# A routed feed-forward on one core: wider slots between the steps of a chunk, and result rows scattered to their tokens by each tile where they were fetched by each chunk

## The chip, the cores and the metric

The kernel runs on one core of one Trainium2 chip. The metric is the device time of one execution in microseconds (us), and the number compared is the median of several runs. Engines: PE is TensorE (PEld its weight loads), DVE VectorE, ACT ScalarE, POOL GpSimd, SP SyncE, which here only issues transfers (SPq is its queue).

## The reference, cut

```python
# x (16,2,104,104), txt (16,512,128); all float32
h = tokenizer(x, gamma, beta, W, b)           # 4 half-patch shifts beside x: 10 planes, normed,
                                              # 8x8 patches -> 169 tokens of 128 per image
h = concatenate([h, txt], axis=1)             # 16 x 681 tokens
z = layernorm(h)
y = p_t * cumsum(p_s * z, axis=1)             # decays per channel along the tokens
h = h + (y @ mix_w.T + mix_b)
z = layernorm(h)
logits = z @ Wg                               # 8 experts
topw, topi = top_k(logits, 2); topw = softmax(topw)
gu = z @ Wgu[e] + bgu[e]                      # for an expert e: 128 -> 512
eo = (silu(g) * u) @ Wd[e] + bd[e]            # 256 -> 128
out = h + sum over a token's 2 experts of topw * eo
```

## The kernel before

There are 16 x 169 image tokens and 16 x 512 text tokens. A **chunk** is 4 tokens on each partition: 7 image chunks (104 partitions, the last with 2 tokens each) and 16 text chunks (128 partitions), 23 in all. The image stage comes first and fills the first 110 us; POOL's last work there is the decayed sums (line 972).

**Steps of a chunk.** Text chunks are loaded, normed, transposed, decayed and summed along the tokens (`text_*`, `norm1`, `z_*`). For every chunk: `mix` (PE) adds the mixed rows; `mixed`, `mixed_stats`, `mixed_var` (DVE) and `norm2` (POOL, lines 966 and 1012) give the second norm's scale and shift; `x_norm` (ACT, line 894) writes the normed rows x2; `x_T`, `logits` (PE, lines 719 and 587), `top_value`, `top_index`, `routing` (DVE), `gate_exp` (POOL, line 1018), `rank` (PE), `place` (DVE, line 1369) and `weights` (DVE) find each token's two experts, its two gate weights and two rows in a buffer in HBM, `xbuf`, in which the rows of one expert lie together. POOL then scatters the normed rows there, one indirect DMA for each of 4 tokens and 2 experts (`scatter`, line 1034, 180 in all).

**Groups and tiles.** Chunks form groups: chunks 0 to 3, 4 to 10, 11 to 17, 18 to 22. When a group's chunks are all scattered, its rows are worked off in **tiles** of 256 rows of one expert: 20, 32, 35 and 27 tiles, 114 in all. For a tile SP loads 128 KB of rows and 386 KB of weights; PE transposes the rows (`tile_T`, line 765), multiplies by gate and up (`gate_up`, two units), then by down (`down`, both line 587); ACT and DVE do silu and product (lines 912, 1476); ACT copies the result rows out of PSUM (`row_keep`, line 919); SP stores them to `ybuf`.

**Results.** When all tiles of a group are stored, POOL fetches each token's two result rows by indirect DMAs (`gather`, line 1048, 180 in all; a waiting gather holds up all that is behind it on POOL), DVE weights and adds them (`combine`, lines 1485 and 1489) and SP stores the output.

**Order.** All engines run in order through one list written out by hand: iterations of 16 slots. `AT` gives each step its slot: `mix=(2, 5)` says that at iteration i, slot 5, chunk i + 2 is mixed. A chunk moves on by one iteration in 16 slots. The tiles of a group are spread over the slots until the next group can begin:

```python
TILE_FROM = [b * SLOTS + 1 for a, b in GROUPS]
TILE_TO = TILE_FROM[1:] + [TILE_FROM[-1] + 2 * KT[-1]]
```

So tiles begin at slots 65, 177, 289 and 369 (counted from iteration 0), and the last ends at 423. A group's gathers lie 6 slots after its last tile and are spread over the next group's tiles; those of the last group follow the last tile alone. A slot has no time of its own: an engine goes on as soon as its next instruction's semaphores allow.

## Time and profile before

| | |
|---|---|
| median of 3 runs | 821.02 us (817.8 to 824.27) |
| the profiled execution, its whole time | 824.18 us |
| its span, first to last instruction | 822.4 us |
| busy in the span | PE 603.9 us (73%), DVE 430.1 (52%), ACT 264.7 (32%), POOL 498.1 (61%) |
| mean granted TensorE clock | 0.835 |

The busy shares are means over stages that differ. An instruction of the indirect kind on POOL counts as busy for about 1 us, and the time until the next one can be issued stands as idle "<-issue"; both occupy POOL.

### The profile page before, as it was taken

The numbers are of one execution on the slowest core, as the hardware profiler recorded it, in microseconds if no ns is written. First come the engines' busy times: TensorE is split into PE (matmuls) and PEld (weight loads), VectorE is DVE, ScalarE is ACT, GpSimd is POOL, SyncE is SP. The second block draws the span as 40 slices with busy tenths as digits, with TensorE's granted clock in tenths as the row PEclk, the third lists the DMA queues.
The fourth block names the chain that finished last, engine by engine and source line by source line (L and its number), as shares of the span: only waits on it lengthen the run. The fifth ranks groups of instructions, "written<-read, shape, count | busy, mean of one in ns | idle before, by whom it ended". The sixth has DMA issues, their size and how long they took to land.

```text
span 822.4 us, 12791 instructions
## 1 busy us (share of the span) xinstructions
PE 603.9 (73%) x3335; PEld 519.1 (63%) x3335; DVE 430.1 (52%) x1708; ACT 264.7 (32%) x690; POOL 498.1 (61%) x520
## 2 busy tenths in 40 slices
PE   3787645327778788698989986999898969999000
PEld 2687634316567576586878875888787758888000
DVE  4789655343556657265655766355544623445122
ACT  2502122112234432244442543254253324444000
POOL 5602327763655756377677776477777767760674
PEclk9998855557789988698997997899999979999555
DMA  7185000126345533565655663667577768984221
GB/s 152 53 290 148 1 0 26 33 90 186 101 127 153 145 104 106 164 194 150 185 169 154 205 198 106 191 202 218 179 214 235 236 197 257 279 279 147 80 77 61
DMA packets 84597, 125.23 MB, mean 152 GB/s; under 512 B 15044, under 2 KB 57792, under 8 KB 84526
## 3 DMA queue, kind: packets, MB, share of 16 engines
q1 hardware_dynamic: 72526, 101.66, 40.9%
q0 software_dynamic: 11520, 22.35, 9.5%
q10 hardware_dynamic: 480, 0.41, 0.4%
q8 instruction: 28, 0.46, 0.3%
q14 instruction: 43, 0.35, 0.1%
HBM read 84.25 MB, written 43.25 MB: 155 GB/s over the span
## 4 chain that ended last, share of the span: by engine, by line
PE 37%; POOL 21%; DVE 14%; issue 13%; DMA 7%; ACT 3%; SPq 3%; POOLq 0%; DVEq 0%; ACTq 0%
PE gu L587 15%; PE dn L587 11%; POOL gat L1048 8%; POOL xbuf L1034 8%; PE mx L587 5%; POOL rs L966 3%; DMA gat<-ybuf,ypos 3%; PE xTp L765 3%; DMA space<-xbuf 2%; DMA space<-in_x_dram 2%; PE tr L587 2%; ACT x L894 1%; PE tr L719 1%; DVE gat L1485 1%; DVE rec L1268 1%
## 5 line engine op out<-in xcount | busy, mean ns | idle before, releaser
L1034 POOL DMA_INDIRECT xbuf<-x,pos x180 | 186.4, 1035 | 112.9 <-DVE pos L1369 56.0
L587 PE MATMUL gu<-space,wts 128*128 128x256 f32 x912 | 246.0, 410 | 9.1 <-DVE space L1476 9.1
L1476 DVE SCALAR_TENSOR_TENSOR space<-gu,wts,space 128x256 f32<-128x256 f32 x228 | 109.1, 482 | 235.7 <-ACT space L912 173.3
L1048 POOL DMA_INDIRECT gat<-ybuf,ypos x180 | 177.7, 987 | 87.9 <-issue 55.5
L912 ACT ACTIVATE space<-gu,wts 128x256 f32<-128x256 f32 x228 | 109.1, 479 | 305.7 <-PE gu L587 305.3
L587 PEld LDWEIGHTS gu<-space,wts 128*128 128x128 f32 x912 | 174.8, 206 | 32.0 <-DVE space L1476 10.9
L587 PEld LDWEIGHTS dn<-wts,space 128*128 128x128 f32 x912 | 127.9, 204 | 14.1 <-DVE space L1476 7.1
L587 PE MATMUL dn<-wts,space 128*128 128x128 f32 x912 | 129.1, 288 | 5.8 <-DVE space L1476 5.8
L765 PE MATMUL xTp<-cst,space 128*128 128x128 f32 x228 | 51.8, 311 | 40.2 <-DMA space<-xbuf 38.1
L765 PEld LDWEIGHTS xTp<-cst,space 128*128 128x128 f32 x228 | 26.7, 154 | 52.6 <-DMA space<-xbuf 40.8
L966 POOL TENSOR_TENSOR rs<-ve,nhalf 128x4 f32<-128x4 f32 (+2 forms) x39 | 40.4, 1036 | 29.7 <-DVE ve L1281 15.2
L906 ACT COPY space<-xTp 128x256 f32<-128x256 f32 x114 | 41.5, 364 | 17.5 <-PE xTp L765 17.5
L919 ACT COPY space<-dn 128x256 f32<-128x256 f32 x114 | 43.7, 383 | 9.4 <-PE dn L587 9.4
L1485 DVE SCALAR_TENSOR_TENSOR gat<-gat,w,space 128x128 f32<-128x128 f32 x64 | 18.2, 346 | 51.8 <-DMA gat<-ybuf,ypos 51.8
L587 PE MATMUL dn<-bdt,ones_r 2*128 2x256 f32 x114 | 44.7, 392 | 0.0
L966 POOL TENSOR_TENSOR irs<-ive,nhalf 104x4 f32<-104x4 f32 (+1 forms) x8 | 7.9, 993 | 46.5 <-DVE ive L1186 43.0
L587 PE MATMUL mx<-mask,tri_r 128*128 128x32 f32 (+2 forms) x23 | 8.5, 368 | 35.6 <-DVE mask L1321 35.6
L587 PE MATMUL mx<-mixT,yT 128*128 128x128 f32 x128 | 32.5, 397 | 2.7 <-DVE need_i L1381 1.7
L587 PEld LDWEIGHTS mx<-mixT,yT 128*128 128x128 f32 x128 | 31.1, 327 | 4.4 <-issue 2.0
L719 PE MATMUL tr<-cst,x 128*128 128x128 f32 (+1 forms) x90 | 19.3, 354 | 17.6 <-ACT x L894 17.6
L894 ACT ACTIVATE x<-space,sh,rs 128x128 f32<-128x128 f32 x64 | 26.4, 487 | 15.0 <-POOL sh L1012 15.0
L587 PEld LDWEIGHTS mx<-mask,tri_r 128*128 128x128 f32 (+1 forms) x23 | 5.5, 238 | 40.5 <-DVE mask L1321 39.9
(198 smaller groups left out, 837.8 us busy)
## 6 DMA issues: line engine op xcount, KB each, us to landing
wts<-wall SPq DMA_DIRECT2D x114, 386.0 KB
space<-xbuf SPq DMA_DIRECT2D x114, 128.0 KB, 2.6
ybuf<-space SPq DMA_DIRECT2D x114, 128.0 KB
xbuf<-zero_rows SPq DMA_DIRECT2D x4, 1024.0 KB, 10.5
xt<-in_txt_dram SPq DMA_DIRECT2D x16, 256.0 KB, 3.0
xbuf<-zero_rows SPq DMA_DIRECT2D x32, 128.0 KB
out_dram<-gat SPq DMA_DIRECT2D x16, 256.0 KB
xbuf<-x,pos POOLq DMA_INDIRECT x180
```

Source lines behind the costliest of these rows:

```text
L587: return nc.tensor.matmul(o, l, r, start=a, stop=z_)
L719: last = nc.tensor.transpose(tr_ps[:, j * p:(j + 1) * p], x2[n % NX2][0:p, j * D:(j + 1) * D], ident[0:p, 0:p])
L765: last = nc.tensor.transpose(xT_ps[:, s * P:(s + 1) * P], xrow[k % NX][:, s * D:(s + 1) * D], ident)
L894: last = nc.scalar.activation(x2[n % NX2][0:p, j * D:(j + 1) * D], h1_of(n)[0:p, j * D:(j + 1) * D], ACT.Identity, bias=sh2[0:p, j:j + 1], ...
L906: copy(xT[k % 2], xT_ps[:, 0:SLOT]).then_inc(W.xs_ok, 1)
L912: nc.scalar.activation(sil[q % 3], gu_ps[q % 3][:, 0:SLOT], ACT.Silu, bias=wts[k % NW][:, W_B + t:W_B + t + 1]).then_inc(W.sil_ok, 1)
L919: copy(yrow[k % NYB], dn_ps[k % 2][:, 0:SUB * D]).then_inc(W.y_row_ok, 1)
L966: tt(out_[0:p, 0:w], var[0:p, 0:w], nhalf[0:p, 0:w], ALU.pow).then_inc(done, 1)
L1034: nc.gpsimd.indirect_dma_start(out=xbuf, out_offset=bass.IndirectOffsetOnAxis(pos[0:p, c:c + 1], 0), in_=x2[n % NX2][0:p, m // 2 * D:(m // ...
L1048: nc.gpsimd.indirect_dma_start(out=gat[b][0:p, (k * W4 + j) * D:(k * W4 + j + 1) * D], out_offset=None, in_=ybuf[g], in_offset=bass.Indire ...
L1476: V.scalar_tensor_tensor(hid[q % 4], gu_ps[q % 3][:, SLOT:2 * SLOT], wts[k % NW][:, W_B + HT + t:W_B + HT + t + 1], sil[q % 3], ALU.add, A ...
L1485: last = V.scalar_tensor_tensor(rows[1][j], rows[1][j], wn[1][j], h1_of(n)[0:p, j * D:(j + 1) * D], ALU.mult, ALU.add)
```

## The change

It does four things.

- **The table of slots.** Steps that stood 1 to 3 slots apart now stand mostly 3 to 5 apart. `x_norm` and `gate_exp` go to the next iteration. A chunk's scatters run over 16 slots from its own slot 15 on; a group's tiles begin 8 slots later (73, 185, 297, 377; the last ends at 431).
- **Rows carry their address.** A row of `xbuf` has 130 elements: 128 values, the gate weight, and the number of the row of a new buffer `results` where its result belongs. `x_copy` (ACT) makes the second copy of the chunk's rows, `weights` (DVE) writes weight and number beside them. The padding rows must have a number too: POOL writes numbers into `zero_rows` (`number_pads`), waits until SP has filled the spare rows of `xbuf` with them, and writes other numbers.
- **Tiles scatter.** `row_keep` multiplies by the gate weight (2 instructions for 1), and POOL scatters the scaled rows to `results` (`scatter_rows`, 2 indirect DMAs per tile, 228 in all), 3 tiles behind. SP loads a chunk's two result rows per token with one plain DMA (`load_results`), DVE adds them with two instructions (`combine`), and the output is stored from the tokens' own buffer. The gathers, `places_of_results` and the stores to `ybuf` are gone.
- **Buffers and places.** Row buffers 5 to 12, result buffers 4 to 8, x2 3 to 4, fetch buffers 4 to 3. `text_y` moves from POOL to DVE. `tile_T` waits for rows and weights together.

```diff
-AT = dict(text_load=(5, 8), ... mix=(2, 5), mixed=(2, 6), ... norm2=(2, 9), x_norm=(2, 12),
-          x_T=(1, 2), ... routing=(1, 15), rank=(0, 1), place=(0, 2), weights=(0, 3))
+AT = dict(text_load=(4, 2), ... mix=(2, 4), mixed=(2, 7), ... norm2=(2, 12),
+          x_norm=(1, 0), x_T=(1, 4), ... routing=(1, 14), gate_exp=(0, 2), rank=(0, 10), place=(0, 12), weights=(0, 13))
-TILE_FROM = [b * SLOTS + 1 for a, b in GROUPS]
+TILE_FROM = [b * SLOTS + 9 for a, b in GROUPS]
+SCATTERS_AT = by_slot([(n * SLOTS + 15 + m * (1 if (n + 1) in [b for a, b in GROUPS] else 2), (n, m))
+                       for n in range(CHUNKS) for m in range(2 * width(n))])
+ROW = D + 2
+    results = nc.dram_tensor("results", (RESULT_ROWS, D), F32, kind="Internal").ap()
...
             load_images(1)
-            sp.wait_ge(W.zero_ok, 1)
+            sp.wait_ge(W.spare_ok, 1)
             for g in range(len(GROUPS)):
                 sp.dma_start(xbuf[ROW0[g] + E * CAP[g]:ROW0[g + 1], :].rearrange("(e p s) d -> p e (s d)", e=E, s=SUB),
-                             zero_rows[:, :].unsqueeze(1).to_broadcast([P, E, SUB * D])).then_inc(W.spare, 16)
+                             zero_rows[:, :].rearrange("p (e c) -> p e c", e=E)).then_inc(W.spare, 16)
...
-                wait(sp, W.xTt_ok, k - NX + 1)
-                sp.dma_start(xrow[k % NX].rearrange("p (s d) -> p s d", s=SUB),
-                             xbuf[bass.ds(row, SLOT), :].rearrange("(p s) d -> p s d", s=SUB)).then_inc(xrow_in[k % NX], 16)
                 wait(sp, W.dn_ok, k - NW + 1)
+                if k >= NX:
+                    sp.wait_ge(yrow_out[(k - NX) % NYB], stored_before(k - NX))
+                sp.dma_start(xrow[k % NX], xbuf[bass.ds(row, SLOT), :].rearrange("(p s) d -> p (s d)", s=SUB)
+                             ).then_inc(tile_in[k % NW], 16)
-            def store_tile(k):
...
+            def load_results(n):
+                b, g, p = n % NG, group_of(n), parts(n)
+                if n == GROUPS[g][0]:
+                    for m in range(TILE0[g + 1] - NYB, TILE0[g + 1]):
+                        sp.wait_ge(yrow_out[m % NYB], stored_before(m))
+                wait(sp, W.sum_ok, n - NG + 1)
+                r0 = n * A_CHUNK
+                sp.dma_start(res[b][0:p, 0:2 * width(n) * D].rearrange("p (j c) -> p j c", j=width(n)),
+                             results[r0:r0 + p * 2 * W4, :].rearrange("(p j k) d -> p j (k d)", p=p, k=2)[:, 0:width(n)]
+                             ).then_inc(res_in[b], 16)
...
             def tile_T(k):
-                pe.wait_ge(xrow_in[k % NX], 16 * (k // NX + 1))
+                pe.wait_ge(tile_in[k % NW], 48 * (k // NW + 1))
...
-                copy(yrow[k % NYB], dn_ps[k % 2][:, 0:SUB * D]).then_inc(W.y_row_ok, 1)
+                for s in range(SUB):
+                    last = nc.scalar.activation(yrow[k % NYB][:, s * D:(s + 1) * D], dn_ps[k % 2][:, s * D:(s + 1) * D], ACT.Copy,
+                                                scale=xrow[k % NX][:, s * ROW + D:s * ROW + D + 1])
+                last.then_inc(W.y_row_ok, 1)
...
-            def gather(n, j, k):
...
+            def scatter_rows(k):
+                pool.wait_ge(W.y_row_ok, k + 1)
+                for s in range(SUB):
+                    place = xrow[k % NX][:, s * ROW + D + 1:s * ROW + D + 2].bitcast(I32)
+                    nc.gpsimd.indirect_dma_start(out=results, out_offset=bass.IndirectOffsetOnAxis(place, 0),
+                                                 in_=yrow[k % NYB][:, s * D:(s + 1) * D], in_offset=None
+                                                 ).then_inc(yrow_out[k % NYB], 16)
+            pool.wait_ge(W.zero_ok, 1)
+            pool.wait_ge(W.seen_zero, 2)
+            number_pads(SPARE_ROW).then_inc(W.spare_ok, 1)
+            pool.wait_ge(W.spare, 16 * len(GROUPS))
+            number_pads(PAD_ROW).then_inc(W.pads_ok, 1)
...
+                    for k, t in units(i, s):
+                        if t == 1:
+                            if k >= 3 and not any(first_of_group(m) for m in range(k - 2, k + 1)):
+                                scatter_rows(k - 3)
+                            if last_of_group(k):
+                                for m in range(k - 2, k + 1):
+                                    scatter_rows(m)
```

**Where the order changes.** First POOL, from the end of the image stage (`space<-space,pow_t` are the decayed sums, `rs`, `sh` are `norm2`, `ex` is `gate_exp`, `xbuf<-x,pos` a scatter). Before, then changed:

```order
L972 TENSOR_TENSOR space<-space,pow_t 128x1040
L966 TENSOR_TENSOR rs<-ve,nhalf 104x4 [waits s_ve2_ok]
L1012 TENSOR_TENSOR sh<-nm,rs 104x4 [waits s_rs2_ok,s_nm2_ok]
L966 TENSOR_TENSOR rs<-ve,nhalf 104x4 [waits s_ve2_ok,s_x2_ok]
L1012 TENSOR_TENSOR sh<-nm,rs 104x4 [waits s_rs2_ok,s_nm2_ok]
L1018 TENSOR_TENSOR ex<-euler,gap 104x4 [waits s_gap_ok]
L1034 DMA xbuf<-x,pos 106496x128 [waits s_x2_ok,s_pos_ok]
```

```order
L991 TENSOR_TENSOR space<-space,pow_t 128x1040
L1063 IOTA zero_rows 128x16 [waits s_seen_zero,s_zero_ok]
L1063 IOTA zero_rows 128x16 [waits s_spare]
L985 TENSOR_TENSOR rs<-ve,nhalf 104x4 [waits s_ve2_ok]
L1031 TENSOR_TENSOR sh<-nm,rs 104x4 [waits s_rs2_ok,s_nm2_ok]
L985 TENSOR_TENSOR rs<-ve,nhalf 104x4 [waits s_ve2_ok,s_x2_ok]
L1031 TENSOR_TENSOR sh<-nm,rs 104x4 [waits s_rs2_ok,s_nm2_ok]
L1037 TENSOR_TENSOR ex<-euler,gap 104x4 [waits s_gap_ok]
L985 TENSOR_TENSOR rs<-ve,nhalf 104x4 [waits s_ve2_ok,s_x2_ok]
L1031 TENSOR_TENSOR sh<-nm,rs 104x4 [waits s_rs2_ok,s_nm2_ok]
L1049 DMA xbuf<-x,pos 106496x130 [waits s_w1_ok,s_meta_ok,s_pos_ok]
```

Two instructions that write `zero_rows`, the second of them behind SP's fills, stand ahead of the first chunk's norm, and the third chunk's norm stands ahead of the first scatter.

Then PE, at the same place (`tr<-cst,x20` transposes x2 of chunk 0, `mx<-mixT` and the line under it mix, `tr<-wg` are the logits, `mx<-mask` and `seen` the ranks). Before, then changed:

```order
L719 MATMUL tr<-cst,x20 128x104 x4
L587 MATMUL mx<-mixT,space 104x128 x4
L587 MATMUL mx<-rows2,ones_r 104x512
L587 MATMUL tr<-wg,x2T 104x8 x4
L587 MATMUL mx<-mask,tri_r 104x32
```

```order
L726 MATMUL tr<-cst,x20 128x104 x4
L596 MATMUL mx<-mixT,space 104x128 x4
L596 MATMUL mx<-rows2,ones_r 104x512
L596 MATMUL tr<-wg,x2T 104x8 x4
L726 MATMUL tr<-cst,x21 128x104 x4
L596 MATMUL mx<-mixT,space 104x128 x4
L596 MATMUL mx<-rows2,ones_r 104x512
L596 MATMUL tr<-wg,x2T 104x8 x4
L596 MATMUL mx<-mask,tri_r 104x32
```

The ranks of chunk 0 now stand behind the transposes and logits of chunk 1 and the mixing of chunk 2.

Last POOL, early in the second group's tiles (`gat<-ybuf,ypos` a gather, `results<-space` a result scatter, `yT` is `text_y`). Before, then changed:

```order
L1004 TENSOR_TENSOR sh<-nm,rs 128x4 [waits s_rs1_ok,s_nm1_ok]
L1034 DMA xbuf<-x,pos 106496x128 x2
L1048 DMA gat<-ybuf,ypos 104x128 [waits s_yrow_out2,s_yrow_out1,s_yrow_out3,s_yrow_out0,s_ypos_ok]
L1034 DMA xbuf<-x,pos 106496x128
L966 TENSOR_TENSOR rs<-ve,nhalf 128x4 [waits s_ve2_ok,s_x2_ok]
L1012 TENSOR_TENSOR sh<-nm,rs 128x4 [waits s_rs2_ok,s_nm2_ok]
L1048 DMA gat<-ybuf,ypos 104x128
L1034 DMA xbuf<-x,pos 106496x128 x3
L1018 TENSOR_TENSOR ex<-euler,gap 128x4 [waits s_w1_ok,s_gap_ok]
L1024 TENSOR_TENSOR yT<-cum,pow_t 128x512 [waits s_mix_ok,s_cum_ok]
```

```order
L1023 TENSOR_TENSOR sh<-nm,rs 128x4
L1057 DMA results<-space 27648x128 x2
L1049 DMA xbuf<-x,pos 106496x130 x2
L1057 DMA results<-space 27648x128 x2
L1049 DMA xbuf<-x,pos 106496x130 x2
L1057 DMA results<-space 27648x128 x2
L985 TENSOR_TENSOR rs<-ve,nhalf 128x4
L1031 TENSOR_TENSOR sh<-nm,rs 128x4
```

Between one norm and the next POOL now issues result scatters in pairs, one pair for each tile, where it issued a gather now and then; `yT` is no longer there.

## Rows read from the trace of the kernel before

**Rows 1.** The page: busy time, share of the span and instructions of each engine.

```profile
PE 603.9 (73%) x3335; PEld 519.1 (63%) x3335; DVE 430.1 (52%) x1708; ACT 264.7 (32%) x690; POOL 498.1 (61%) x520
```

**Rows 2.** Windows: length, busy us of PE, PEld, DVE, ACT, POOL, clock, DMA, GB/s.

```profile
110.00:187.00 77.00, 29.27 (x126) 24.10 (x126) 35.17 (x216) 13.95 (x33) 50.22 (x53) 0.50 0.15 42
187.00:342.00 155.00, 119.35 (x587) 100.80 (x588) 86.66 (x380) 53.42 (x142) 87.61 (x94) 0.82 0.45 134
342.00:514.00 172.00, 153.69 (x813) 130.88 (x811) 102.66 (x446) 70.48 (x191) 126.03 (x130) 0.90 0.57 170
514.00:668.00 154.00, 139.58 (x773) 119.06 (x773) 73.50 (x284) 58.17 (x160) 106.39 (x109) 0.94 0.68 205
668.00:761.00 93.00, 91.28 (x511) 78.34 (x511) 42.14 (x116) 37.32 (x106) 51.70 (x54) 0.96 0.78 242
```

**Rows 3.** Timeline after the last tile: start, length, engine, line, operation, [idle before].

```profile
761.17 0.37 ACT L919 COPY space<-dn 128x256 f32<-128x256 f32 x1 [1.04 <-PE dn L587]
...
764.13 0.95 POOL L1048 DMA_INDIRECT gat<-ybuf,ypos  x1 [27.97 <-DMA ybuf<-space]
...
813.13 0.95 POOL L1048 DMA_INDIRECT gat<-ybuf,ypos  x1 [0.30 <-issue]
...
817.97 0.33 SPq L551 DMA_DIRECT2D out_dram<-gat  x1
```

**Rows 4.** Groups on POOL, 342 to 514 us: busy, mean ns | idle.

```profile
L1034 POOL DMA_INDIRECT xbuf<-x,pos x56 | 58.6, 1046 | 32.9 <-issue 17.8 <-DVE pos L1369 13.9 <-DVE ve L1281 0.9
L1048 POOL DMA_INDIRECT gat<-ybuf,ypos x32 | 33.9, 1059 | 11.2 <-issue 11.2
L966 POOL TENSOR_TENSOR rs<-ve,nhalf 128x4 f32<-128x4 f32 x14 | 14.6, 1044 | 2.6 <-DVE ve L1453 2.2
L1024 POOL TENSOR_TENSOR yT<-cum,pow_t 128x512 f32<-128x512 f32 x7 | 8.9, 1265 | 0.1
```

**Rows 5.** Timeline around the first chunks, POOL and then ACT.

```profile
114.98 1.01 POOL L966 TENSOR_TENSOR rs<-ve,nhalf 104x4 f32<-104x4 f32 x1
...
127.42 1.25 POOL L1034 DMA_INDIRECT xbuf<-x,pos  x1 [1.23 <-DVE pos L1369]
...
116.37 1.65 ACT L894 ACTIVATE x<-h_img,sh,rs 104x128 f32<-104x128 f32 x4 [9.75 <-POOL sh L1012]
...
125.27 1.65 ACT L894 ACTIVATE x<-h_img,sh,rs 104x128 f32<-104x128 f32 x4 [5.70 <-POOL sh L1012]
```

**Rows 6.** Fills of spare rows: SP queue, landing times, a window.

```profile
43.72 7.59 SPq L481 DMA_DIRECT2D xbuf<-zero_rows  x4
...
DMA to landing us min/median/max: 6.6/10.5/12.0
...
48.00:52.00 4.00, 4.00 (x39) 4.00 (x38) 4.00 (x10) 0.00 (x0) 0.00 (x0) 1.00 1.07 372
```

**Rows 7.** Timeline where the first group opens.

```profile
181.99 0.99 POOL L1034 DMA_INDIRECT xbuf<-x,pos  x1 [0.30 <-issue]
...
185.29 0.37 SPq L533 DMA_DIRECT2D space<-xbuf  x1
...
187.30 0.69 PE L765 MATMUL xTp<-cst,space 128*128 128x128 f32 x2 [14.55 <-DMA space<-xbuf]
```

**Rows 8.** Groups on POOL, 187 to 342 us.

```profile
L1034 POOL DMA_INDIRECT xbuf<-x,pos x52 | 54.5, 1048 | 41.2 <-DVE pos L1369 25.2 <-issue 15.7 <-DVE ve L1281 0.3
L966 POOL TENSOR_TENSOR rs<-ve,nhalf 128x4 f32<-128x4 f32 (+1 forms) x14 | 14.3, 1022 | 13.5 <-DVE ve L1453 8.4 <-DVE ve L1281 4.9
...
L1018 POOL TENSOR_TENSOR ex<-euler,gap 128x4 f32<-128x4 f32 (+2 forms) x7 | 7.0, 993 | 5.9 <-DVE gap L1307 5.8
```

**Rows 9.** Groups on POOL, 514 to 668 us.

```profile
L1048 POOL DMA_INDIRECT gat<-ybuf,ypos x55 | 55.0, 1000 | 20.4 <-issue 16.5 <-DMA ybuf<-space 3.8
L1034 POOL DMA_INDIRECT xbuf<-x,pos x40 | 40.6, 1014 | 27.1 <-DVE pos L1369 15.6 <-issue 11.4
```

**Rows 10.** Landing of the text loads, 256 KB each, line 475.

```profile
DMA to landing us min/median/max: 2.8/3.0/3.5
```

254 lines of the change are left out of this document (104 added, 150 removed).

## The prediction, made before the run

> **What bounds the kernel now.** The page's busy line comes first, since it says which engines can be a bound at all: PE 603.9 us of 822.4, POOL 498.1 [rows 1]. Neither is full over the span, so the next view is windows cut by stage [rows 2]. The reader is to see five stretches. From 110 to 187 us there is no tile: PE 29 of 77 us at a granted clock of 0.50, POOL 50. From 187 to 342 us (first group's 20 tiles) PE 119 of 155. From 342 to 514 (32 tiles) PE 154 of 172, POOL 126. From 514 to 668 (35 tiles) PE 140 of 154, POOL 106. From 668 to 761 (27 tiles) PE 91 of 93: PE is the bound. What follows is a tail without PE: the last result row is copied by 761.54, the first of 40 gathers starts at 764.13, the last at 813.13, the last store at 817.97 [rows 3]. So 60.9 us stand behind the last tile, and POOL alone sets them.
>
> What POOL's busy time hides is shown by its groups: beside 92.5 us for 88 indirect DMAs stand 29.0 us of "<-issue" [rows 4]. An indirect DMA thus occupies POOL for 1.05 + 0.33 = 1.38 us in this stretch; alone in the tail it is (813.13 - 764.13) / 39 = 1.256 us [rows 3]. True waits of POOL from 342 to 514 us are only 13.9 + 0.9 + 2.2 = 17.0 us [rows 4]: it is taken for 155 of 172 us, as much as PE. This is the number on which the rest hangs.
>
> **The change, part by part.** The sum is made against the profiled execution's span, 822.4 us.
>
> *The wait for the fills.* POOL now writes numbers, waits until SP's four fills of 1.06 MB have landed, and writes again, all ahead of chunk 0's norm, which started at 114.98, right behind the image sums [rows 5]. SP issued the fills at 43.72, hidden beside the image stage [rows 6]; now it can't before about 115, and everything from the first norm on is queued behind POOL's wait: ACT's x_norm, PE's transposes, DVE's routing. Price: SP took 7.59 us to issue four, the last issue began near 48.4 (it took the rest of the 7.59), and the slowest landed 12.0 us after issue, so at most 48.4 + 12.0 - 43.72 = 16.7 us; 4.26 MB at the 372 GB/s of the window beside them is 11.5 us [rows 6]. I take **+15**, near the upper end, since issue and landing add to the bytes.
>
> By the Trainium skill (DMA: Bandwidth & Descriptors, section on the anatomy of one DMA on the SWDGE path) a transfer costs about 2.0 us plus its bytes over 436 GB/s; for all four as one this is an estimate of 11.8 us, and the sum would be 3 us lower. The landing of 12.0 us for one of four [rows 6] speaks for more.
>
> *The spacing before the first tile.* Chunk 0's ranks now stand on PE behind chunk 1's transposes and logits and chunk 2's mixing, and its first scatter behind chunk 2's norm on POOL. In this stretch chunks follow each other in turns of 125.27 - 116.37 = 8.9 us [rows 5]; norm to first scatter took 127.42 - 114.98 = 12.4 us. The first scatter comes almost a turn later, **+8** (0 if the chunks overlap fully, 10 if the opening waits for weights too). From there to the last scatter before the tiles (127.42 to 182.98, [rows 5, 7]) POOL has the same 32 scatters and is nearly always taken, so no gain there; then 4.3 us to PE's first transpose [rows 7], as before.
>
> *The three stretches with chunks and tiles.* PE's work is what it was. POOL's changes: result scatters come in (2 per tile), gathers go, `text_y` goes to DVE, which is busy half the time and hides 0.7 us more per chunk. ACT's second instruction per tile and `x_copy` lie beside 822.4 - 264.7 = 558 us in which ACT is idle [rows 1]; nothing.
> First stretch: POOL waited 25.2 + 0.3 + 8.4 + 4.9 + 5.8 = 44.6 us [rows 8], so it was taken for 110.4. Now + 40 x 1.35 (1.048 + 15.7/52) = 54.0, less 7 x 1.27 = 8.9 for `text_y`: 155.5 us, all of the stretch. The wider slots take PE's waits away, but not this; with an imperfect fit **+5** (-3 at 1.256 us each, +15).
> Second: 155 taken, + 32 x 1.38 = 44.2, - 8.9 = 190.3 us against a stretch of 172 and PE work of 154: POOL becomes the bound. With 3 us in which it starves while a group opens, **+21** (+3 if each of the 120 costs 1.256; +35 if the old 17 us of waits stay).
> Third: waits 3.8 + 15.6 = 19.4, taken 134.6, + 15 x 1.30 = 19.5, - 2 x 1.27 = 2.5, so 151.6 of 154 [rows 9]; PE needs 140. Two engines so near each other don't overlap fully: the second stretch of before had 155 and 154 and took 172. I take 158, **+4** (-2, +17).
> Fourth: 54 scatters x 1.256 = 68 us of 93, hidden behind PE; 0. The bytes are the same: gathers of 64 KB become loads, stores become scatters.
>
> What the page on the same subject says (section "Issuing engine by pattern": simple stores from Sync, indirect ones from GPSIMD, and first-byte latencies of about 1 and 0.6 us) speaks against this change: it takes 114 plain stores from SP, which is not the bound, and makes 228 indirect ones on POOL. By the Trainium skill's 1 us for each, the 48 more would be an estimate of 48 us; by the rows' 1.256 to 1.38 they are 60 to 66 us of POOL.
>
> *The tail.* The last copy ends about 0.4 us later (two instructions), two scatters 2.5 us, landing to SP's next issue 185.29 - 182.98 = 2.3 us [rows 7]: 766.7. A load of 512 KB: 256 KB took 3.0 us [rows 10], I take 4: 770.7; its sum 1.5: 772.2. The fourth load waits for that sum (three buffers): 776.2, the fifth 1.5 later, sum at 779.2, and 822.4 - 817.97 = 4.4 us from the last store to the end as before [rows 3]: 783.6. Behind the last tile stand 22 us for 60.9: **-39** (-35 if the loads share bandwidth, -42 if they take 3 us).
>
> Sum: 822.4 + 15 + 8 + 5 + 21 + 4 - 39 = **836.4 us**. The profiled execution took 1.8 us more than its span, so 838.2 against its 824.18, a ratio of 1.017; times the median of 821.02 this is **835 us**.
>
> **The rivals.**
> *POOL packs tightly (faster).* The wide slots let each engine run ahead, the deeper buffers keep POOL fed, and an indirect DMA costs 1.256 us. The stretches give -3 + 3 - 2 = -2, the fill 11.5, the spacing 2, the tail -39: 795 us of span, 794 as a median. For it: that price is what the tail and, nearly, 668 to 761 us show. Against it: beside busy DVE and norms each group of rows shows 1.30 to 1.38 [rows 4, 8, 9], and each group's opening leaves POOL without results for some tiles. It decides for "faster" when middle, fill and spacing together give no more than 31. Chance 0.13.
> *A draw.* Waits vanish in the first and third stretch as fast as scatters come: middle +15, spacing 3, fill 15, tail -39: 816 of span, 815. Chance 0.20.
> *The openings grow (still slower).* A group's tiles can't begin until the last chunk's scatters have landed, and those stand one slot apart between pairs of result scatters, 15 indirect DMAs or 20 us in 8 slots that held 12 us of PE work. PE drains, idles 10 us instead of 4 at each of three openings, its clock falls to the lower level of 1.2 GHz (0.50 is granted in the stretch where PE is busy 29 of 77 us, [rows 2]), and the norms come late on ACT: middle +50, 856 of span, 855. For it: POOL is the bound just there. Chance 0.17.
> *The change doesn't widen anything.* The wide slots may be without effect, since an engine that is full sets the pace in any table; this is part of my forecast, not a time of its own.
>
> **How the numbers follow.** The forecast, 825 to 848, has 0.50. A measurement of this kernel tells about 1% from no change, so the bounds are 813 and 829. Below 813: the first rival, 0.13. Between: the draw and a little of the forecast's lower end, 0.22. Above: 0.65. All bounds together would reach from about 794 to 870; the range leaves out one in ten at each side: 811 to 856.
>
> **What the changed profile would show.** POOL: nothing but a wait on the fills from about 115 to 130 us, and the first scatter near 150, not 127. First tile near 210. Between 342 and 514 of before: POOL without true waits, about 190 us long, PE's idle time ending on "POOL sh" through ACT. Idle before result scatters put down to "issue". The last tile near 815, and 22 us behind it. The forecast is wrong if an indirect DMA costs much less than 1.3 us when they come in pairs, if the fills are waited for under 10 us, or if PE was held in the first stretch by waits that the wide slots remove and POOL has slack that the means hide.

## The result and the profile after

The changed kernel takes **858.07 us** as a median of 4 runs (855.13 to 859.51), beside 820.66 us for the kernel before in the same runs (4 runs, 817.8 to 824.27): a ratio of 1.0449 (95%: 1.0398 to 1.05). It is slower, as forecast, but by 37 us where the forecast had 14, and 2 us above the upper end of the range. The profiled execution took 855.13 us, its span 853.0 us, which is 30.6 us more than the 822.4 us of before. The account below is of these 30.6 us; the other 6.5 of the 37 lie in how far each profiled execution stands from its median (2.9 us under for after, 3.5 us over for before).

The page's busy line, to be read beside [rows 1]:

```profile
PE 608.5 (71%) x3335; PEld 520.1 (61%) x3335; DVE 398.0 (47%) x1580; ACT 304.1 (36%) x827; POOL 522.6 (61%) x555
```

PE has the same instructions and nearly the same busy time, POOL 24.5 us more. The loss is idle time. To place it, the span is cut where each group's first transpose starts on PE. These are the four of after, from PE's timeline:

```profile
209.56 0.69 PE L771 MATMUL xTp<-cst,space 128*128 128x128 f32 x2 [16.73 <-DMA bdt<-bias]
...
374.49 0.69 PE L771 MATMUL xTp<-cst,space 128*128 128x128 f32 x2 [11.76 <-DMA bdt<-bias]
...
570.46 0.69 PE L771 MATMUL xTp<-cst,space 128*128 128x128 f32 x2 [15.68 <-DMA bdt<-bias]
...
737.27 0.69 PE L771 MATMUL xTp<-cst,space 128*128 128x128 f32 x2 [27.00 <-DMA bdt<-bias]
```

In the kernel before, the first of them started at 187.30, with 14.55 us of PE's idle time ahead of it, the number in brackets [rows 7]. The other three:

```profile
336.55 0.69 PE L765 MATMUL xTp<-cst,space 128*128 128x128 f32 x2 [3.94 <-DMA space<-xbuf]
...
511.80 0.69 PE L765 MATMUL xTp<-cst,space 128*128 128x128 f32 x2 [3.89 <-DMA space<-xbuf]
...
666.70 0.69 PE L765 MATMUL xTp<-cst,space 128*128 128x128 f32 x2 [4.23 <-DMA space<-xbuf]
```

I call these four points the openings, and the time from one to the next a stretch. The differences against the forecast:

| part | before | after | difference | forecast |
|---|---|---|---|---|
| to the first transpose of group 1 | 187.30 | 209.56 | +22.3 | +23 |
| first stretch | 149.25 | 164.93 | +15.7 | +5 |
| second stretch | 175.25 | 195.97 | +20.7 | +21 |
| third stretch | 154.90 | 166.81 | +11.9 | +4 |
| fourth, to the end of the last copy | 94.84 | 94.26 | -0.6 | 0 |
| tail | 60.9 | 21.5 | -39.4 | -39 |
| span | 822.4 | 853.0 | +30.6 | +14 |

Windows cut at these points (columns as in [rows 2], the clock third from the right):

```profile
110.00:209.50 99.50, 31.04 (x138) 25.73 (x136) 34.64 (x216) 17.16 (x39) 50.18 (x55) 0.50 0.41 115
209.50:374.50 165.00, 126.52 (x583) 104.21 (x583) 79.90 (x388) 61.55 (x168) 114.56 (x124) 0.77 0.38 116
374.50:570.50 196.00, 154.47 (x819) 130.74 (x819) 96.58 (x428) 81.88 (x230) 146.15 (x156) 0.86 0.53 156
570.50:737.30 166.80, 135.03 (x761) 115.65 (x761) 66.20 (x248) 67.93 (x198) 118.25 (x122) 0.89 0.63 191
737.30:831.50 94.20, 91.48 (x513) 78.12 (x513) 34.99 (x68) 44.53 (x135) 51.54 (x54) 0.97 0.77 243
831.50:853.00 21.50, 0.00 (x0) 0.00 (x0) 6.83 (x10) 0.02 (x1) 3.16 (x4) 0.51 0.56 195
```

The bracket values of the three later openings add up to 54.4 us, where before they made 12.1: PE stands still 42 us more there, and the three stretches are 48.3 us longer in sum. The last line against the tail of [rows 3] is the gain: 21.5 us behind the last copy.

**The fills.** POOL's timeline where [rows 5] stood:

```profile
115.30 0.18 POOL L1063 IOTA zero_rows<- 128x16 int32 x1
130.30 0.16 POOL L1063 IOTA zero_rows<- 128x16 int32 x1 [14.82 <-DMA xbuf<-zero_rows]
130.43 1.01 POOL L985 TENSOR_TENSOR rs<-ve,nhalf 104x4 f32<-104x4 f32 x1
...
151.00 1.22 POOL L1049 DMA_INDIRECT xbuf<-x,pos  x1 [1.48 <-issue]
...
202.60 0.99 POOL L1049 DMA_INDIRECT xbuf<-x,pos  x1 [0.30 <-issue]
```

The norm of the first chunk starts at 130.43, not 114.98, which is 15.4 us later. The first scatter starts at 151.00, 20.6 us behind that norm where it was 12.4 before (+8.1). The last scatter ahead of the tiles ends at 203.59, 52.6 us behind the start of the first, where it was 55.6 (-3.0). The first transpose follows 6.0 us later, where it was 4.3 (+1.6). These four make the +22.3.

**POOL's groups**, first the first stretch (beside [rows 8]), then the second ([rows 4]), then the third ([rows 9]):

```profile
L1049 POOL DMA_INDIRECT xbuf<-x,pos x52 | 53.9, 1036 | 23.4 <-issue 18.4 <-DVE x L1374 4.7 <-DVE ve L1452 0.3
L1057 POOL DMA_INDIRECT results<-space x37 | 36.2, 980 | 11.7 <-issue 11.2 <-ACT space L932 0.5
L985 POOL TENSOR_TENSOR rs<-ve,nhalf 128x4 f32<-128x4 f32 (+1 forms) x14 | 14.7, 1047 | 19.1 <-DVE ve L1303 16.8 <-DVE ve L1452 2.1
...
L1057 POOL DMA_INDIRECT results<-space x65 | 65.5, 1008 | 20.3 <-issue 19.3 <-DVE x L1374 0.3 <-DVE ve L1452 0.3
L1049 POOL DMA_INDIRECT xbuf<-x,pos x56 | 55.4, 989 | 23.8 <-issue 17.8 <-DVE x L1374 6.0
L985 POOL TENSOR_TENSOR rs<-ve,nhalf 128x4 f32<-128x4 f32 x14 | 15.6, 1115 | 3.4 <-DVE ve L1303 3.0 <-DVE ve L1452 0.2
...
L1057 POOL DMA_INDIRECT results<-space x70 | 68.8, 982 | 21.7 <-issue 19.8 <-ACT space L932 1.5 <-DVE ve L1303 0.3
L1049 POOL DMA_INDIRECT xbuf<-x,pos x40 | 40.3, 1008 | 22.7 <-issue 13.3 <-DVE x L1374 9.4
...
L985 POOL TENSOR_TENSOR rs<-ve,nhalf 128x4 f32<-128x4 f32 x4 | 4.2, 1041 | 3.5 <-DVE ve L1303 3.5
```

An indirect DMA takes (68.8 + 19.8) / 70 = 1.27 us to (53.9 + 18.4) / 52 = 1.39 us of POOL. The part of it called issue, 0.28 to 0.35 us for each, is in no busy share. In the second stretch all true waits are 0.3 + 0.3 + 6.0 + 3.0 + 0.2 = 9.8 of 196 us: POOL is full, as forecast. In the first they are 4.7 + 0.3 + 0.5 + 16.8 + 2.1 = 24.4 us, of which 5.9 lie ahead of 209.5: 18.5 of 165. In the third they are 1.5 + 0.3 + 9.4 + 3.5 = 14.7 of 166.8. Windows of the first stretch say where its waits lie:

```profile
209.50:230.00 20.50, 15.19 (x58) 12.18 (x59) 9.03 (x47) 5.58 (x15) 6.38 (x7) 0.63 0.47 146
230.00:250.00 20.00, 17.77 (x83) 14.88 (x83) 10.33 (x48) 7.19 (x20) 12.08 (x15) 0.79 0.42 118
...
270.00:290.00 20.00, 17.12 (x86) 14.34 (x85) 11.12 (x55) 9.24 (x25) 16.03 (x17) 0.86 0.41 127
...
350.00:374.50 24.50, 9.51 (x36) 7.42 (x36) 6.42 (x21) 5.91 (x17) 17.65 (x19) 0.59 0.30 89
```

POOL is idle two thirds of the first 20 us, since the next chunk's norm waits for DVE and there are no results yet. From about 250 us it is full, and in the last 24.5 us PE works for 9.5 only, because it waits for POOL.

**The last opening.** POOL's timeline (an `xbuf` scatter brings rows to the tiles about to open, a `results` scatter takes finished rows away), SP's, PE's:

```profile
724.82 0.97 POOL L1049 DMA_INDIRECT xbuf<-x,pos  x1 [0.31 <-issue]
726.09 0.95 POOL L1049 DMA_INDIRECT xbuf<-x,pos  x1 [0.30 <-issue]
727.35 0.96 POOL L1057 DMA_INDIRECT results<-space  x1 [0.30 <-issue]
728.61 0.96 POOL L1057 DMA_INDIRECT results<-space  x1 [0.31 <-issue]
729.88 0.96 POOL L1049 DMA_INDIRECT xbuf<-x,pos  x1 [0.30 <-issue]
...
733.15 0.35 SPq L545 DMA_DIRECT2D space<-xbuf  x1
...
709.88 0.38 PE L596 MATMUL dn<-bdt,ones_r 2*128 2x256 f32 x1
```

PE has finished group 3 at 710.3 and does nothing until 737.27. The last of the chunk's scatters issues at 729.88, and among the indirect DMAs ahead of it stand result scatters that nothing waits for. From the `xbuf` scatter's end to SP's load are 733.15 - 730.84 = 2.3 us, as before [rows 7]. From there to the first transpose are 4.1 us, where it was 187.30 - 185.29 = 2.0.

The profile names `bdt<-bias` as the releaser. It is the last of the three loads of the tile, for all of which `tile_T` now waits; before it waited for the rows alone. At the four openings the first transpose stands 3.6 to 4.1 us behind SP's first load, where it stood 2.0 to 2.1 us behind it, and the first `gate_up` 6.7 to 7.5 us, where it stood 5.4 to 6.0. So this wait costs about 1.3 to 1.5 us at each opening. The forecast has no term for it, and no run takes it back alone.

### The profile page after: what moved, and what is told of

It reads as the page before. It is cut to its first block, busy times and chain, and to the rows that moved or that the text cites. A ratio compares the mean times of both kernels' runs of the same rounds, so it can differ in the third digit from the quotient of the medians.

```text
span 853.0 us, 12864 instructions
## 1 busy us (share of the span) xinstructions
PE 608.5 (71%) x3335; PEld 520.1 (61%) x3335; DVE 398.0 (47%) x1580; ACT 304.1 (36%) x827; POOL 522.6 (61%) x555
## 4 chain that ended last, share of the span: by engine, by line
PE 35%; POOL 28%; issue 14%; DVE 10%; DMA 7%; SPq 3%; ACT 2%; POOLq 0%; DVEq 0%; ACTq 0%
PE gu L596 15%; POOL xbuf L1049 12%; POOL results L1057 10%; PE dn L596 10%; PE mx L596 3%; PE xTp L771 3%; POOL rs L985 3%; DMA bdt<-bias 2%; POOL ex L1037 2%; DMA space<-in_x_dram 2%; DMA xbuf<-zero_rows 1%; PE tr L596 1%; DMA xbuf<-x,pos 1%; DMA res<-results 1%; DVE recs L1133 1%
## 5 line engine op out<-in xcount | busy, mean ns | idle before, releaser
L1057 POOL DMA_INDIRECT results<-space x228 | 224.3, 984 | 97.0 <-issue 59.8
L1049 POOL DMA_INDIRECT xbuf<-x,pos x180 | 182.1, 1011 | 81.5 <-issue 61.2
L596 PEld LDWEIGHTS gu<-space,wts 128*128 128x128 f32 x912 | 177.2, 208 | 25.9 <-issue 3.0
L596 PEld LDWEIGHTS dn<-wts,space 128*128 128x128 f32 x912 | 125.5, 200 | 17.3 <-DVE space L1475 10.5
L771 PE MATMUL xTp<-cst,space 128*128 128x128 f32 x228 | 53.9, 321 | 86.1 <-DMA bdt<-bias 79.5
L932 ACT ACTIVATE space<-dn,space 128x128 f32<-128x128 f32 x228 | 72.6, 377 | 7.7 <-PE dn L596 6.5
L726 PE MATMUL tr<-cst,x 128*128 128x128 f32 (+1 forms) x90 | 18.7, 345 | 68.8 <-ACT x L899 68.8
L726 PEld LDWEIGHTS tr<-cst,x 128*128 128x128 f32 (+1 forms) x90 | 12.8, 179 | 73.3 <-ACT x L899 71.8
L596 PE MATMUL mx<-mixT,yT 128*128 128x128 f32 x128 | 33.9, 427 | 11.9 <-DVE yT L1482 11.9
L888 ACT ACTIVATE z<-xt,sh,rs 128x128 f32<-128x128 f32 x64 | 26.4, 489 | 24.1 <-POOL sh L1023 24.1
L899 ACT ACTIVATE x<-h_img,sh,rs 104x128 f32<-104x128 f32 x26 | 10.8, 483 | 63.2 <-POOL sh L1031 63.2
```

What stands on the lines that cost most here:

```text
L596: return nc.tensor.matmul(o, l, r, start=a, stop=z_)
L726: last = nc.tensor.transpose(tr_ps[:, j * p:(j + 1) * p], x2[n % NX2][0:p, j * ROW:j * ROW + D], ident[0:p, 0:p])
L771: last = nc.tensor.transpose(xT_ps[:, s * P:(s + 1) * P], xrow[k % NX][:, s * ROW:s * ROW + D], ident)
L888: last = nc.scalar.activation(z[:, j * D:(j + 1) * D], xt[b % NXT][:, j * D:(j + 1) * D], ACT.Identity, bias=sh1[:, j:j + 1], scale=rs1[:, ...
L899: last = nc.scalar.activation(x2[n % NX2][0:p, j * ROW:j * ROW + D], h1_of(n)[0:p, j * D:(j + 1) * D], ACT.Identity, bias=sh2[0:p, j:j + 1 ...
L932: last = nc.scalar.activation(yrow[k % NYB][:, s * D:(s + 1) * D], dn_ps[k % 2][:, s * D:(s + 1) * D], ACT.Copy, scale=xrow[k % NX][:, s * ...
```

## Experiments

The first four: two kernels mend one thing each, one takes the new table out of the changed kernel, and one puts it alone into the kernel before. Ten more follow from what these showed. "After" is the changed kernel, and every ratio is to the kernel before.

**early_fill**: the numbering of the spare rows stands ahead of the image stage on POOL.

```diff
             tt(rows2[:, :], rows2_raw, rows2_hi.bitcast(F32), ALU.subtract).then_inc(W.rows_ok, 1)
+            pool.wait_ge(W.zero_ok, 1)
+            pool.wait_ge(W.seen_zero, 2)
+            number_pads(SPARE_ROW).then_inc(W.spare_ok, 1)
```

> The changed kernel with the first numbering of the spare rows moved ahead on POOL, to before the image stage, so that SP can fill the spare rows beside that stage again; all else as it is. My theory: POOL's 14.8 us of waiting for the fills lie wholly on the path, so the time falls by about 14 to 15 us, to 843 us (ratio to the kernel before 1.027), and the first tile's transposes come at about 195 us instead of 209.6. Rival: something else (the weights' tables, which SP also builds later now, or the pace of the image chunks) would have held the first group anyway: less than 5 us are gained.

Measured: 840.54 us, ratio 1.0214 (1.0177 to 1.0251), 17.5 us less than after. The second numbering no longer waits, and the norm stands at 115.49:

```profile
115.33 0.17 POOL L985 IOTA zero_rows<- 128x16 int32 x1
115.49 1.01 POOL L993 TENSOR_TENSOR rs<-ve,nhalf 104x4 f32<-104x4 f32 x1
```

The first transpose starts 14.4 us earlier, at 195.15. Of this 11.6 us are left at the last opening and 10.9 in the profiled span (842.1), so the medians' 17.5 overstate it a little or the profiled execution understates it. The wait costs about what the forecast said, and it is a matter of where one instruction stands.

**held**: result scatters that fall in the eight slots with a group's last scatters are issued behind them.

```diff
+def held(at):
+    for a, b in GROUPS[:-1] + GROUPS[-1:]:
+        first = (b - 1) * SLOTS + 15
+        if first <= at < first + 8:
+            return first + 8
+    return at
```

> The changed kernel with one edit: result scatters that fall into the 8 slots in which the last chunk of a group is scattered are held back until those 8 scatters are out; the number of instructions is the same. Theory of the openings: between the first and the last of the last chunk's scatters stand 12 result scatters at the third opening (15 us) and 2 to 6 at the others; they move behind. PE's idle time before the last group falls from 27 to about 12 us, and since the last stretch has POOL time to spare this is kept: about 843 us in all. Rival, POOL's throughput alone: the work is only put in another order, PE waits for it elsewhere, and less than 5 us are gained.

Measured: 839.96 us, ratio 1.0219 (1.018 to 1.0258), 18.1 us less than after. The eight scatters of the last chunk now stand together on POOL (line 1079 is the `xbuf` scatter):

```profile
704.86 0.96 POOL L1079 DMA_INDIRECT xbuf<-x,pos  x1 [0.30 <-issue]
...
713.70 0.96 POOL L1079 DMA_INDIRECT xbuf<-x,pos  x1 [0.30 <-issue]
714.96 0.96 POOL L1087 DMA_INDIRECT results<-space  x1 [0.31 <-issue]
```

The three stretches are 2.9, 6.0 and 8.5 us shorter than after's, and PE's idle time ahead of the three openings is 10.0, 10.7 and 19.3 us. The order at the openings is worth 18 us. I had expected the last idle time to fall to about 12 us, by a wrong count: in after only six result scatters, not 12, stand between the first and the last of the chunk's scatters (713.46 to 729.88), which is 7.6 us, and the idle time fell by 7.7. The rest of it stays, because POOL reaches the first of these eight scatters 3.2 us after PE has finished the group, and the eight take 10 us themselves. That part is POOL's load.

**old_spacing**: the changed kernel with the slots of the kernel before.

```diff
-AT = dict(text_load=(4, 2), text_stats=(3, 0), ...
+AT = dict(text_load=(5, 8), text_stats=(4, 3), ...
-TILE_FROM = [b * SLOTS + 9 for a, b in GROUPS]
+TILE_FROM = [b * SLOTS + 1 for a, b in GROUPS]
```

> The result scatters, addresses in rows and buffers of the changed kernel, but with the table of slots of the kernel before (steps 1 to 3 slots apart, scatters at slots 3 to 13, tiles 8 slots earlier). Theory (both parts cost): the spacing's 8 us before the first tile and some 10 us at the openings go, the fill wait and the POOL load stay: about 838 to 842 us. Rival 1, the wide slots are what keeps POOL fed under its new load: without them the time rises above 865 us. Rival 2, the spacing is neutral: 855 to 860 us.

Measured: 852.94 us, ratio 1.0372 (1.0336 to 1.0409), 5 us less than after, where I expected 15 to 20. Openings at 208.35, 376.11, 573.73 and 733.67, with 6.8, 6.3 and 8.8 us of idle time on PE ahead of the later three. So with the old slots the openings are short, but the stretches (167.8, 197.6, 159.9) lose little in sum: against old_spacing the wide slots cost the changed kernel +1.2 us to the first opening, -2.8 and -1.7 in the first two stretches and +6.9 in the third, where PE's idle time is 27.0 and not 8.8 us. Idle time at an opening shows that POOL is late, and not by itself what the lateness costs.

The 8 us of spacing before the first tile nearly vanish here. The first scatter does come earlier, at 144.31 and not 151.00, but the last one ends at 202.35, only 1.2 us earlier: with the old slots POOL waits for DVE three times for 1.6 us, and the scatters take 58.0 us, not 52.6.

**spacing_only**: the kernel before with the new slots, `text_y` still on POOL.

```diff
-AT = dict(text_load=(5, 8), ...
+AT = dict(text_load=(4, 2), ...
-SCATTER_SLOTS = (3, 4, 6, 7, 8, 11, 12, 13)
+SCATTERS_AT = by_slot([...])
```

> The kernel before, with gathers and all its buffers, and only the new table of slots (with the scatters at their new slots and the tiles 8 slots later). Theory (both parts cost): 8 us more before the first tile, some 5 to 12 us more at the openings, the tail as long as before: 834 to 842 us. Rival, the wide slots take waits away where POOL isn't full: 815 to 825 us. With the run of the result scatters under the old table this tells whether the two parts add: the sum of their two differences to the kernel before against the 37 us of the whole.

Measured: 847.85 us, ratio 1.0299 (1.0257 to 1.034), above what I expected. Taken with old_spacing it made no sense as a sum: 27 us for the slots and 31 for the rest, against 37 together. POOL's groups in its first stretch showed a confound of my own:

```profile
L1033 POOL TENSOR_TENSOR yT<-cum,pow_t 128x512 f32<-128x512 f32 x7 | 8.8, 1261 | 34.5 <-DVE cum L1477 34.5
```

In the new table `text_y` stands one slot behind the sums that DVE makes for it, and as a POOL instruction it holds up every scatter behind it.

**spacing_dve**: the same with `text_y` on DVE, as the change has it.

```diff
-                tt(yT[:, :], cum[:, :], pow_t[:, REV + T_IMG:REV + T], ALU.mult).then_inc(W.y_ok, 1)
+                V.tensor_tensor(yT[:, :], cum[:, :], pow_t[:, REV + T_IMG:REV + T], ALU.mult).then_inc(W.y_ok, 1)
```

> The kernel before with the new table of slots, as in the run with the table alone, and text_y on DVE as in the changed kernel. In the run with the table alone POOL waited 34.5 us in the first stretch for the text sums, which stand one slot ahead of text_y in the new table. If that wait was what cost 26 us, this one comes to 832 us or less (the 8 us before the first tile stay). Rival: the wide spacing costs by itself, through PE's clock and the order of steps: 842 us or more.

Measured: 824.71 us, ratio 1.0044 (1.0012 to 1.0077), within the theory's 832 or less: **the wide slots, with `text_y` on DVE, are nearly free in sum**. No run has the old slots and `text_y` on DVE in the kernel before, so these figures hold for the pair. Openings at 194.70, 350.20, 522.79 and 667.78, so +7.4 us to the first one, +6.3 in the first stretch, -2.7 in the second, -9.9 in the third, +1.8 behind it. Its windows show what the first stretch pays:

```profile
194.70:350.20 155.50, 126.92 (x582) 105.01 (x583) 81.58 (x389) 53.41 (x141) 79.70 (x87) 0.76 0.41 125
...
522.80:667.80 145.00, 134.01 (x761) 114.83 (x761) 71.29 (x281) 57.37 (x159) 102.89 (x106) 0.95 0.72 218
```

The granted clock of the first stretch is 0.76 with the wide slots and 0.82 in [rows 2], and the same matmuls take 126.9 us, not 119.4. After has 0.77 (PE busy 126.5 us), old_spacing 0.82 (117.4): the clock goes with the slots, not with the result scatters. That it sets the length of the stretch doesn't follow: old_spacing has the higher clock and the longer first stretch, 167.8 against 164.9 us. Against this kernel the rest of the change is +14.9 us to the first opening, +9.4, +23.4 and +21.8 in the stretches, and -41.8 from the last opening to the end.

**direct**: result rows leave by one plain SP store for each tile, in tile order.

```diff
-                                scatter_rows(k - 3)
...
+                                store_tile(k - 2)
```

> The changed kernel without its 228 result scatters: SP stores each tile's scaled rows in the order of the tiles with one plain DMA, and the chunks load whatever rows stand at their numbers, so the routing of results back to tokens is left out. POOL issues 180 indirect DMAs in place of 408. My theory (POOL is the bound of the second stretch and nearly of the others): the three stretches fall from 165, 196 and 167 us to about 155, 170 and 152, in all about 805 us. Rival: the stretches are long because of the new order of steps and of PE's lower clock, and the scatters only fill time that is there: 835 us or more.

Measured: 798.55 us, ratio 0.9734 (0.9679 to 0.979). Against after the three stretches lose 6.5, 25.9 and 21.2 us, 53.6 in sum, and the idle times ahead of the openings are 6.6, 5.7 and 6.0 us. In the second stretch POOL now waits for its inputs 22.7 + 41.3 + 1.0 us, where it had been full:

```profile
L1060 POOL DMA_INDIRECT xbuf<-x,pos x56 | 58.3, 1041 | 39.6 <-DVE x L1378 22.7 <-issue 16.9
L996 POOL TENSOR_TENSOR rs<-ve,nhalf 128x4 f32<-128x4 f32 x14 | 16.5, 1179 | 42.5 <-DVE ve L1307 41.3 <-DVE ve L1456 1.0
```

That is the price of the result scatters in the middle, and it agrees with the remainder from spacing_dve (9.4 + 23.4 + 21.8 = 54.6) by a quite different edit. The theory had the stretches right within 7 us (158, 170 and 146) and the sum 6 us too high.

It also answers two rivals. Direct keeps everything else of the change (the longer rows, ACT's second instruction, the buffers, the wait for weights), and its stretches of 158.4, 170.1 and 145.6 us are within 3 us of spacing_dve's 155.5, 172.6 and 145.0; so these parts cost next to nothing in sum. And direct has no gathers, spacing_dve has them: in the second stretch POOL waits 65.0 us here and 27.4 us there, so it is taken for 105 and for 145 us, and the stretch is equally long. After has it taken for 186, and the stretch is 196. So POOL's load cost nothing up to 145 us in this stretch; at 186 it is more than the stretch was, and sets its length.

**early_held**: both mends, as in the two diffs above.

> The changed kernel with both mends: the spare rows numbered before the image stage, and result scatters held behind the last chunk's scatters. The two act at different places, one before the first tile and one at the openings, so my theory is that they add, 17 and 18 us: 822 to 825 us, no faster and no slower than the kernel before. Rival: what is saved ahead is lost again to a lower PE clock or to POOL's pace: 832 us or more.

Measured: 824.01 us, ratio 1.0045 (1.0012 to 1.0078), 34 us less than after: 17.5 + 18.1 = 35.6, so they add up within 2 us, as expected. With both, the changed kernel is where the kernel before is.

**norms_dve**: `norm1`, `norm2` and `gate_exp` leave POOL, each with a product in place of its power.

```diff
-                tt(ex[0:p, 0:w], euler[0:p, 0:w], gap[0:p, 0:w], ALU.pow).then_inc(W.ex_ok, 1)
+                V.tensor_tensor(ex[0:p, 0:w], euler[0:p, 0:w], gap[0:p, 0:w], ALU.mult).then_inc(W.ex_ok, 1)
```

> The changed kernel with the chunk steps norm1, norm2 and gate_exp on DVE in place of POOL, at the same slots; since the power is not computed there, each takes a product in its place, so norms and gate weights have other values and tokens go to other experts (the number of tiles and of transfers is fixed). All 408 indirect DMAs stay. It takes 30, 30 and 11 us of work off POOL in the three stretches. Theory of the full POOL: the second stretch falls by 25 us or more, the others by 5 to 11: 810 to 820 us. Rival, latency of the chain of steps: the norms get faster by about 1 us each and no more: 845 us or more.

Measured: 780.85 us, ratio 0.9518 (0.9462 to 0.9575), 77 us less than after. I expected half of that. By stages it is 28.4 us to the first opening (181.19) and 10.1, 23.2 and 12.7 in the stretches. So more than a third of it lies where there is no result scatter: the first norm no longer stands behind POOL's wait for the fills. A power of 128x4 numbers takes POOL 1.04 us, and the norm stands between scatters in program order. To see how much a kernel with the true values keeps, three kernels compute them.

**newton_after, newton_mended, newton_before**: both norms on DVE by three Newton steps, 11 instructions; then the same with both mends; then the same in the kernel before.

```diff
+                then(V.tensor_scalar(a.bitcast(I32), v.bitcast(I32), 1, None, ALU.logical_shift_right))
+                then(V.tensor_scalar(y.bitcast(I32), a.bitcast(I32), -1.0, 1597463007.0, ALU.mult, ALU.add))
+                for r in range(3):
+                    then(V.scalar_tensor_tensor(a, y, -0.5, y, ALU.mult, ALU.mult))
+                    then(V.tensor_tensor(a, a, v, ALU.mult))
...
```

> The changed kernel with norm1 and norm2 on DVE, this time with their true values: the inverse root by a bit shift, a subtraction and three Newton steps, 11 small DVE instructions for one of POOL. gate_exp stays on POOL. It takes 14 x 1.6 = 22 us off POOL in each of the first two stretches, but a norm now takes some 2.5 us of DVE, not 1.2 us of POOL. The run with products instead came to 781 us. Theory: nearly all of that gain was that norms no longer queue behind scatters on POOL, so this comes to 785 to 800 us. Rival: the gain was the work taken off POOL (gate_exp's part is back, a quarter) and the short chain: 810 us or more.

> The same norms on DVE, together with both mends (early numbering of the spare rows, result scatters held behind the last chunk's). If everything adds, 17 us of the fill's wait and some of the 18 us of the openings come off the run with the norms alone: 765 to 780 us, faster than the kernel before by 5%. Rival: with the norms off POOL, the openings are short already and the hold brings nothing: 780 to 785.

> The kernel before with norm1 and norm2 on DVE in the same way, and nothing else of the change. It tells whether the norms' place on POOL is a fault of the changed kernel alone. Theory (POOL taken for 155 of 172 us in the second stretch there too, norms behind scatters before the first tile): it gains as well, but less than half as much as the changed kernel does, to 795 to 808 us. Rival: POOL has room there and the Newton steps make the chain longer: 820 us or more.

Measured: 829.88 us, ratio 1.0103 (1.005 to 1.0156); 812.55 us, 0.9885 (0.9832 to 0.9938); 807.04 us, 0.9841 (0.9785 to 0.9896). The first two are misses by 30 us and more, and the first lies where its rival had it (810 or more); the third is as expected. Real norms on DVE give the changed kernel 28 us, not 77, and in it the early numbering no longer moves the first opening (191.63 against 191.72). What differs from norms_dve are 10 more instructions per norm in a chain on DVE, and `gate_exp`, still on POOL.

**free_after, free_mended, free_before**: `gate_exp` leaves POOL too, as a silu on ACT.

```diff
+                nc.scalar.activation(ex[0:p, 0:w], gap[0:p, 0:w], ACT.Silu).then_inc(W.ex_ok, 1)
...
-                tt(ex[0:p, 0:w], euler[0:p, 0:w], gap[0:p, 0:w], ALU.pow).then_inc(W.ex_ok, 1)
```

> The changed kernel with norm1, norm2 on DVE (Newton steps) and gate_exp on ACT: silu of the gap of the two logits, which DVE divides by the gap to get the second gate weight; true values throughout. POOL has nothing left between the scatters. Theory (an instruction that stands between scatters on POOL holds them back until its input is there, and is held back by them): gate_exp's move brings most of the 49 us between the run with products (781) and that with Newton steps alone (830): 785 to 798 us. Rival: the products were fast because the chain of a norm was 2 us shorter in each turn; then this stays at 815 us or more.

> The same with both mends of before (early numbering of the spare rows, held result scatters). The mends took 17 us off with Newton steps alone (830 to 813). Theory: the fill's wait no longer stands ahead of any norm, so only the last opening's part stays: 775 to 790 us, the fastest so far. Rival: the mends bring nothing once POOL is free: as the run without them.

> The kernel before with the norms on DVE and gate_exp on ACT, gathers and its tail of 61 us kept. Theory: less of its time hung on POOL's order, so it gains a few us over the 807 with the norms alone: 797 to 805 us, and the version with result scatters and both mends is now ahead of it, since its tail of 22 us stays. Rival: it gains as much as the other, 785 us or less, and the result scatters never pay.

Measured: 818.62 us, ratio 0.9957 (0.9932 to 0.9982); 806.80 us, 0.9807 (0.9765 to 0.9848); 812.49 us, 0.9877 (0.9836 to 0.9918). All three missed upward, and the first lies where its rival had it, that of the short chain (815 or more). My theory, that POOL's power instructions were the whole of it, falls: POOL has none in the chunks now, and it waits for DVE instead. POOL's scatters between first and third opening, in free_after and in norms_dve:

```profile
L1038 POOL DMA_INDIRECT xbuf<-x,pos x108 | 111.1, 1028 | 115.3 <-DVE x L1359 86.3 <-issue 28.9
```

```profile
L1027 POOL DMA_INDIRECT xbuf<-x,pos x108 | 109.0, 1009 | 89.1 <-DVE x L1346 58.6 <-issue 30.5
```

POOL waits for DVE 27.7 us longer in free_after, and these two stretches are 352.3 us long there and 327.6 in norms_dve, 24.7 us more. My reading is that with POOL free the chain on DVE that leads up to a scatter sets the pace, and that it is longer by the Newton steps. newton_before and free_mended, 807.04 and 806.80 us, are the fastest kernels here that compute all; their intervals (0.9785 to 0.9896, and 0.9765 to 0.9848) overlap, so it is a tie. Side by side, free_mended is 5.7 us ahead of free_before, as I had expected, and newton_mended 5.5 us behind newton_before: whether the change pays once both mends are in hangs on the rest of the kernel.

## Why the forecast had the direction and not the size

**Right, with their size.** The wait for the fills: +15 forecast, POOL waited 14.82 us, and early_fill took 14.4 us off the first opening. The spacing before the first tile: the first scatter came +8.1 us later behind its norm, for +8. That the row "to the first transpose" has +22.3 for +23 is in part luck: the scatters then took 3.0 us less, where the forecast said "no gain there", and the opening 1.6 us more, where it said "as before". Nor is the +8 a price of the spacing alone: spacing_dve has +7.4, but with its first norm itself 2.6 us late, and the old slots give the changed kernel only 1.2 us back. The tail: -39, measured -39.4; five loads and sums behind the last tile, as worked out. The fourth stretch: 0, measured -0.6. POOL as the bound in the second stretch: 186 us taken of 196 (forecast 190.3), +20.7 for +21, and direct shows that the result scatters are the cause.

**Wrong in size: "First stretch ... with an imperfect fit +5".** The taken time was not the fault: 165 - 18.5 = 146.5 us, less than the 155.5 forecast (37 result scatters at 1.28 us, not 40 at 1.35). The fault is to set the stretch's length to POOL's work with 44.6 us of waits thought away (3.0 of them lie ahead of 187 us, in the pause before the first tile, so that the taken time of before was 113.4, not 110.4). Of the waits 18.5 us stayed, most of them at the start, where no result is there to scatter and the next norm waits for DVE. POOL's list is in order, so later work can't move there. The step that failed is thus the "imperfect fit" of 5 us; the runs showed +15.7. The result scatters cost 6.5 us of it by direct (9.4 by the remainder from spacing_dve). What the wide slots do to it depends on the kernel: +6.3 us in the kernel before with `text_y` on DVE, -2.8 in the changed kernel, where POOL waits 18.5 us in this stretch, and 23.1 with the old slots. So the two parts don't add up here. The lower clock and PE's 7 to 9.5 us more of busy time are there with the wide slots and not with the old ones, but no run changed the clock alone, and old_spacing speaks against it as the cause in the changed kernel.

**Wrong in size: "Third ... I take 158, +4".** Here POOL's taken time was forecast to the point (151.6; 166.8 less waits of 14.7 is 152.1), and the surcharge of 4 us for two engines that don't overlap was too small: the runs showed +11.9. It lies at the opening, 27.00 us in one piece. With the old slots the changed kernel's third stretch is 159.9 us, +5.0, about what I forecast; the wide slots add the other 6.9 at the opening, and holding six result scatters back takes 8.5 away (held). The forecast had no term for the order there. In the other direction the figures are +21 to 22 us for the result scatters (direct and spacing_dve) and -9.9 for the wide slots in a kernel without them.

**The nearer rival.** "The openings grow" named this mechanism and its place, with 855 us: middle +50, measured +48.3. Part of that nearness is luck: held puts the order of the scatters there at 18 us, and the rest of the 48.3 is POOL's load, which direct takes away. I gave it 0.17 and took the forecast's +30, although both rested on the same full POOL: when an engine is full ahead of a point that the others wait for, its backlog shows there. Two points of the rival were off. PE idled 12 to 27 us, not 10. And the clock doesn't suffer more from the longer pause: in the 7.8 us behind the last opening it was 0.61, then 1.00; in the kernel before it was 0.50 in as many us, and then 1.00 as well. After, then before:

```profile
737.20:745.00 7.80, 5.98 (x21) 4.72 (x22) 0.97 (x2) 1.84 (x5) 2.88 (x3) 0.61 0.82 295
745.00:755.00 10.00, 10.00 (x59) 8.63 (x58) 2.90 (x6) 4.58 (x14) 3.74 (x4) 1.00 0.56 173
```

```profile
666.70:674.50 7.80, 5.46 (x16) 4.15 (x17) 0.56 (x2) 1.58 (x4) 5.97 (x7) 0.50 0.95 310
674.50:684.50 10.00, 10.00 (x59) 8.63 (x58) 5.34 (x15) 3.98 (x11) 7.56 (x9) 1.00 0.75 232
```

**What the parts are worth**, from runs: fills 11 to 17.5 us, order at the openings 18.1, result scatters 54 in the middle (in which the 18.1 lie) against some 39 to 42 gained behind the last opening, wide slots 4 (spacing_dve) to 5 (old_spacing), in different stretches. The two mends take 34 of the 37 us away.

**Open.** Why norms_dve stands 38 us below free_after. The longer chain on DVE is argued from POOL's waits; but in norms_dve other values also send tokens to other experts, and no run separates the two. Nor was the clock tried by itself, nor `tile_T`'s wait for the weights, nor `text_y` on DVE with the old slots in the kernel before.

## What to carry to other kernels

Count an in-order engine's issue time with its busy time, and then ask where in a stretch its work can lie: waits at the start stay, and the backlog comes out at the next point that others wait for, so work that nobody needs soon should stand behind the instructions that open a stage. An initialization whose transfers were hidden needs its trigger as early as before, or all that its engine has queued behind it waits for the transfer. Load on an engine that still waits was free here: the second stretch was equally long with POOL taken for 105 and for 145 us. At 186 us POOL set the length, and the stretch was 23 to 26 us longer. Moving plain stores to indirect ones on such an engine cost 54 us here for 228 of them, more than the 39 us of tail that they saved; and a combination of two single-part kernels can mislead, as `text_y` did, when a part relies on another one.
